# Edge lists in blocks of 16 columns, cut to a multiple of 32 columns

## What is computed

```python
h = (x_flat @ W_gat).reshape(M, HEADS, NUM_EXPERTS)        # 4 heads, 4 experts
a_src = (h * att_src).sum(-1)
a_dst = (h * att_dst).sum(-1)
e = leaky_relu(a_src[src] + a_dst[dst], negative_slope=0.2)
e_max = segment_max(e, dst, num_segments=M)
ee = exp(e - e_max[dst])
denom = segment_sum(ee, dst, num_segments=M)
alpha = ee / (denom[dst] + 1e-16)
msg = h[src] * alpha[:, :, None]
agg = segment_sum(msg, dst, num_segments=M) + b_gat
```

## Time and profile before

| | before |
|---|---|
| median of 3 runs | 3209.75 us (3207.09 to 3212.43) |
| the profiled execution's own time | 3207.62 us |
| its span | 3205.9 us |
| busy in the span: PE / DVE / ACT / POOL | 1521.4 / 1561.3 / 545.2 / 811.7 us |
| the loop of gathers L1559 | 512 transfers, 1197.9 to 1839.4 us |
| pairs of windows in use | 9, that is 18 windows of 32 columns, 576 columns |

### The profile page before, as it was taken

The page is one execution under the profiler, slowest core; times in us unless marked ns, Lnnn a source line. Parts: engine busy times, 40 slices in busy tenths (PEclk is TensorE's granted clock), DMA queues, the critical chain, the costliest instruction groups (busy, mean ns, idle before and its releaser), DMA issues.

```text
span 3205.9 us, 20219 instructions
## 1 busy us (share of the span) xinstructions
PE 1521.4 (47%) x6554; PEld 735.1 (23%) x6554; DVE 1561.3 (49%) x2668; ACT 545.2 (17%) x858; POOL 811.7 (25%) x875
## 2 busy tenths in 40 slices
PE   0011113968673000000000012869976999699969
PEld 0011111642232000000000000244464222244443
DVE  8999995365646042222222226464146555520065
ACT  0000001024211000000000002413023555310033
POOL 0000005720003747777777761000000000000000
PEclk6555555558695555555555555869965999799979
DMA  9000001000005101111111100010000000000000
GB/s 399 26 0 0 0 13 35 14 9 0 6 17 11 57 10 18 18 18 18 18 18 18 18 13 2 1 21 1 0 1 3 1 1 1 6 0 1 1 0 27
DMA packets 70842, 65.78 MB, mean 21 GB/s; under 512 B 50449, under 2 KB 64609, under 8 KB 68321
## 3 DMA queue, kind: packets, MB, share of 16 engines
q1 hardware_dynamic: 43712, 54.60, 6.0%
q0 software_dynamic: 27040, 10.02, 3.3%
HBM read 21.96 MB, written 40.50 MB: 19 GB/s over the span
## 4 chain that ended last, share of the span: by engine, by line
PE 42%; DVE 26%; POOL 20%; issue 9%; ACT 2%; DMA 1%; POOLq 0%; DVEq 0%; SPq 0%
POOL rows L1559 15%; PE bank L840 13%; DVE keys L1806 12%; PE bank L516 8%; PE bank L558 7%; POOL rows L1549 2%; POOL tok_end L1564 2%; POOL scratch_start L1541 2%; PE bank L540 2%; DVE n_tok L396 1%; DVE mean L394 1%; PE bank L503 1%; DVE var L403 1%; PE bank L479 1%; DVE n_tok L413 1%
## 5 line engine op out<-in xcount | busy, mean ns | idle before, releaser
L1559 POOL DMA_INDIRECT rows<-scratch_row,idx_ring x512 | 485.8, 949 | 188.8 <-issue 155.7
L750 DVE TENSOR_TENSOR hid<-hid,bank 128x512 f32<-128x512 f32 (+1 forms) x320 | 273.9, 898 | 282.2 <-PE bank L540 281.5
L1222 PE MATMUL bank<-ident,last 128*20 128x128 f32 x3 | 0.8, 409 | 853.2 <-DVEq L1420 853.2
L1806 DVE TENSOR_TENSOR keys<-keys 128x1024 f32<-128x1024 f32 (+1 forms) x388 | 353.6, 953 | 7.5
L516 PE MATMUL bank<-n_chan,weights_odd 64*128 64x512 f32 x896 | 279.0, 710 | 106.6 <-ACT hid L627 106.0
L627 ACT ACTIVATE hid<-bank,weights_odd 128x512 f32<-128x512 f32 x448 | 282.9, 684 | 253.9 <-PE bank L516 253.5
L1678 POOL DMA_INDIRECT keys<-scratch_sorted,weights_odd x128 | 125.3, 979 | 537.4 <-DVEq L1859 495.8
L558 PE MATMUL bank<-hid,weights_odd 128*64 128x512 f32 x896 | 249.2, 638 | 0.5 <-DVE hid L750 0.5
L1709 PE MATMUL bank<-ident,keys 128*128 128x128 f32 x224 | 55.1, 428 | 370.3 <-DVEq L1774 370.3
L840 PE MATMUL bank<-image,diag 128*128 128x512 f32 x512 | 223.5, 595 | 1.2 <-DVE image L812 1.2
L1378 DVE TENSOR_TENSOR keys<-rows,a_dst_e 128x128 f32<-128x128 f32 x18 | 5.5, 307 | 439.3 <-DMA rows<-scratch_row,idx_ring 439.0
(11 more groups left out here) (416 smaller groups left out, 2263.9 us busy)
## 6 DMA issues: line engine op xcount, KB each, us to landing
scratch_sums<-n_tok SPq DMA_DIRECT2D x12, 2048.0 KB, 36.0
rows<-scratch_row,idx_ring POOLq DMA_INDIRECT x576, 2.4
scratch_sums<-sums SPq DMA_DIRECT2D x18, 384.0 KB, 2.3
scratch_start<-n_tok SPq DMA_DIRECT2D x2, 2048.0 KB, 9.0
a_dst_e<-scratch_start SPq DMA_DIRECT2D x1, 4096.0 KB, 13.3
keys<-scratch_sorted,weights_odd POOLq DMA_INDIRECT x136, 2.3
n_chan<-in_x SPq DMA_DIRECT2D x1, 2048.0 KB, 8.1
edge_i<-in_L_ffn_edge_index SPq DMA_DIRECT2D x1, 2048.0 KB, 13.4
```

The lines of the kernel that those rows point to most:

```text
L750: v.tensor_tensor(blocks, blocks, bank[4 + b][:, :].unsqueeze(1).broadcast_to([P, KS, 512]), ALU.mult).then_inc(S("scaled"), 1)
L1559: g.indirect_dma_start(out=rows[:, b, c, :], out_offset=None, in_=row_d[:, :], in_offset=at(idx_ring[:, b, c:c + 1])).then_inc(s_gath[b], 16)
L1806: m = v.tensor_tensor(o, p, q, op)
```

## The change

`WIN` goes from 32 to 16. All buffers of a window are sized by it and all loops and waits follow. The number of pairs in the whole memory, `NW // 2`, goes from 32 to 64. The two other edits only keep the eight transfers that bring the sorted list in (L1684) at 256 columns each.

```diff
-WIN = 32
+WIN = 16
...
-            g.iota(list_r, pattern=[[4, 8]], base=0, channel_multiplier=0, allow_small_or_imprecise_dtypes=True).then_inc(S("c_made"), 1)
+            g.iota(list_r, pattern=[[EPP // (16 * WIN), 8]], base=0, channel_multiplier=0, allow_small_or_imprecise_dtypes=True).then_inc(S("c_made"), 1)
...
-                g.indirect_dma_start(out=sorted_e[:, 8 * WIN * w:8 * WIN * (w + 1)].bitcast(F32), out_offset=None, in_=runs, in_offset=at(list_i[:, w:w + 1])).then_inc(S("list_in"), 16)
+                g.indirect_dma_start(out=sorted_e[:, EPP // 8 * w:EPP // 8 * (w + 1)].bitcast(F32), out_offset=None, in_=runs, in_offset=at(list_i[:, w:w + 1])).then_inc(S("list_in"), 16)
```

## The result

| | before | after |
|---|---|---|
| median of 4 runs | 3208.42 us (3206.22 to 3212.43) | 3175.55 us (3173.58 to 3178.65) |
| profiled execution | 3207.62 us, span 3205.9 | 3174.07 us, span 3172.4 |

The ratio is 0.9897, interval 0.988 to 0.9914: faster by 1.0%, a gain of 32.9 us where 42.9 were forecast. The time lies 0.55 us above the range that was given. The direction and nearly every term of the sum were right; one term, the loop, was off by 11 us. The kernel was measured twice more, with gains of 35.5 and 28.6 us, so the place just outside the range is a matter of chance: the second of the three times, 3171.99 us, lies inside it. The loop's extra time is in all three traces.

The account below looks back on a forecast made before the run. The number of GpSimd's transfers was taken to set the time from 1001.5 us to the loop's end, VectorE only at its start and end. Terms -40.0 - 1.9 + 1.0 - 2.0 = -42.9 us gave 3167 us, range 3160 to 3175.

Parts of the forecast that it names:

- the loop: GpSimd's 512 gathers at L1559: 641.5 us as before, plus 1.0 us for more collisions with VectorE's L1390.
- 32 gathers fewer: Ahead of L1551: 64 transfers of L1549 become 32 at 1.249 us each, moving everything behind forward, -40.0 us.
- window 0: VectorE's first window, ahead of the first loop gather: 34 steps stay but at half size, -1.9 us of 12.4.
- last window and its store: End of the stage, ahead of tok_end: window -1.9 us, store of 192 KB in place of 384 KB -0.1, together -2.0.
- empty turns: Loop turns without work, 47 in place of 23 on four engines: hidden, 0 us; GpSimd's end 2 us before the store lands.
- the handshake: VectorE's index copy to GpSimd's next gathers in the loop: slack 8 us in each of 32 turns, so hidden.
- the lead: GpSimd's queue reads 14.0 us ahead of its engine, still whole with windows of 16; +11.6 us if it were nil.
- Rival C: In the loop VectorE cannot keep up and GpSimd waits for L1399's copy each turn: above 3210 us, chance 1%.
- D: The change does not shorten the lists; 32 gathers only move from ahead of L1551 into the loop: 3207 us, chance 1%.
- Rival A: GpSimd's empty turns ahead of tok_end come into the open: up to 11.6 us, 3170 to 3179 us, chance 8%.
- the costs' end of 3172: Slow end of the forecast's unknown costs: windows with no shrinking and +2.5 us in the loop give 3172 us.
- three signs: Forecast wrong if L1559 waits for VectorE inside the loop, only its own queue releases tok_end, or TensorE's later stages change time.

## Why the prediction missed

| step | forecast, us | traces, us |
|---|---|---|
| 32 gathers fewer | -40.0 | -39.9 |
| window 0 | -1.9 | -2.1 |
| the loop | +1.0 | +12.1 |
| last window and its store | -2.0 | -2.5 |
| empty turns | 0 | 0 |
| variation ahead of L1549 and behind tok_end | | -1.1 |
| sum | -42.9 | -33.5 |

The last line but one is -5.5 ahead of L1549 and +4.4 from the first tok_end to the end, both in stages whose instructions are the same.

**Right: the gathers.** 32 x 1.249 us, and nothing else was late next at L1551: its engine stood still for only the usual 0.30 us ahead of it.

**Right: the windows, the handshake and the lead.** Windows took 10.3 to 10.9 us (10.7 forecast), and VectorE waited for rows 311.3 us in 32 windows, 9.7 each. GpSimd never waited for VectorE beyond the start (the second of its two waits is a usual 0.3 us). Rival C was nowhere near; D is excluded by the 32 and 512 transfers.

**Right in its result, wrong in a number: the empty turns.** Branches of the 47 turns on GpSimd's and VectorE's queue:

```profile
L1554 POOLq COMPARE_BRANCH  x47: 50/50/50, 1789.0 to 1809.4; - x47
...
L1408 DVEq COMPARE_BRANCH  x47: 62/63/63, 1816.8 to 1850.3; - x47
```

GpSimd's take 20.4 / 46 = 0.443 us each, not 0.586 as in the earlier trace rows; VectorE's 33.5 / 46 = 0.728, as there. GpSimd's loop body was halved by the change (32 transfers in place of 64) and VectorE's was not, and only the pace of the first moved: an empty turn costs by the length of the body that is skipped. That is an inference from these two rows. They ended at 1809.8, and tok_end's own row in the result shows that the store ended its wait, at about 1818.3: 8.5 us of cover, where 2 were forecast. The lead held: the turns began at 1788.6, 14.4 us before the last gather, where 14.0 were taken. (The price of a lead of nil is 27.6 - 15.7 = 11.9 us and not 11.6.) Rival A didn't happen on this chip. VectorE's turns hid as said: L1461 waited 38.71 us for tok_end, where 39 were left by the working.

**Wrong: the term "The loop", by 11.1 us.** The step that failed is the sentence that twice as many windows with operations half as long give something between 0 and another 2.5 us. It scaled the excess of the rows before with count and length, and it put gaps at nothing. The excess goes by neither. A gather that begins while L1390 runs is held until 0.2 us before its end and then takes its usual 0.94. In the kernel before:

```profile
1283.94 1.22 DVE L1390 TENSOR_TENSOR keys<-rows,scale 128x512 f32<-128x512 f32 x1 [0.54 <-ACT scale L1238]
1284.86 1.06 POOL L1559 DMA_INDIRECT rows<-scratch_row,idx_ring  x1 [0.31 <-issue]
```

L1390 takes 1.22 us, but a gather begins 0.91 into it, so 1.22 - 0.91 - 0.2 = 0.11 us is lost, nearly every time. After, L1390 takes 0.68 us and a gather begins 0.21 into it: 0.68 - 0.21 - 0.2 = 0.27, and measured 0.29. A shorter operation, with its start shifted against the row of gathers, costs nearly three times as much each time, and 27 times in place of 16. The prediction's own rows would have given the bound: they make L1390 0.70 us long at half size, so up to 0.70 - 0.2 = 0.50 us in each of 32 windows, 16 us, and not 2.5. With that end the range would have held the time. As it stood, 3175 was the costs' end of 3172 plus 3 for the runs' spread, and nothing of rival A, though the text counts a part of it in. The other half, 6.5 us of gaps, had no row in the loop before. There was a hint outside it: the 128 gathers of L1678 have one gap of 3.2 us too, in both kernels, at number 113. Why the gaps come stays open. Of the three signs that the prediction named for being wrong none came; what it expected to see did fail at one place, the 0.3 us between all the gathers of L1559.

On the rule of the Trainium skill that the prediction weighed (SBUF — State Buffer, the "DVE blocks DMA" trap): it gave up to +20 us and the trace's own value was taken, +1.0. The measured 5.6 us lies between. The rule's box names operations in a mode that uses two ports, such as a copy in float32; here a multiply and scans in float32 with two inputs held the gathers. The runs agree that a gather is kept waiting until close to the operation's end; that a shared port does it, no run here shows.

## What to carry to other kernels

If one engine's long row of short transfers sets the time, a collision with another engine's operation is to be priced by phase: for each operation, where in it the next transfer begins, with its whole length as the upper bound. When a change alters lengths the phase is new, and a row of before gives the mechanism, not the size. A tiny delay may be worth more than a faster operation (two added copies of 0.19 us gave 8.6 us back). The shortest way to less time was fewer transfers: each column is 1.25 us here.

## What the hardware showed beyond that

- The making of descriptors for an indirect transfer that begins beside a VectorE scan of two inputs takes nearly as long as the scan: 4.15 us beside scans of 4.43, 0.94 once they had ended. A gather that had begun 0.33 us before the multiply was not held: 0.94 us.
- The row of gathers has a pause of 2 us (1.7 above the usual) behind number 112 and every 112th after it with blocks of 16 and 28, in the changed kernel in all three traces. Eight transfers more ahead of the loop did not move it, and a lead of the queue of 14.4 us in place of 8.1 did not remove it. With blocks of 20, 32 and 34 there is none. Its cause stays open.
- Two of the four chips on record took 5% longer for the same kernel (3379 and 3384 against 3206 and 3207 us), and the change's parts had other prices there: 1.0203 for short blocks alone, where the count of gathers is unchanged.
